# The small embedding of a graph recommender is added to the rows of x by GpSimd, in 26 pieces between steps of the sort

## The reference

```python
def _propagate(all_emb, rows, cols, vals):
    acc = all_emb
    x = all_emb
    for _ in range(N_LAYERS):
        x = jax.ops.segment_sum(vals[:, None] * x[cols], rows, num_segments=N_NODES)
        acc = acc + x
    return acc / (N_LAYERS + 1)
...
light_out = _propagate(all_emb, graph_rows, graph_cols, graph_vals)
mm_out = _propagate(mm_all, graph_rows, graph_cols, graph_vals)
users_emb = all_users[users] + _upsample_nearest(mm_users[users])
items_emb = all_items + _upsample_nearest(mm_items)
rating = users_emb @ items_emb.T + bias_user[users] + bias_item.T
return sigmoid(rating)
```

## Time and profile before

| | us |
|---|---|
| median of 3 runs | 5368.86 |
| lowest, highest | 5368.59, 5371.43 |
| profiled execution, its own time | 5364.2 |
| its span in the trace | 5362.3 |

### The profile page before, as it was taken

How to read it: one execution, slowest core, us unless ns; L and a number is a source line. 1 busy time by engine, 2 the same in 40 slices (tenths; PEclk the granted TensorE clock), 3 DMA queues, 4 the chain that set the end, 5 groups by cost and what they waited for, 6 DMA issues and landing times.

```text
span 5362.3 us, 195922 instructions
## 1 busy us (share of the span) xinstructions
PE 3360.9 (63%) x71235; PEld 2862.9 (53%) x71473; DVE 4779.3 (89%) x7551; ACT 2466.3 (46%) x4385; POOL 2473.0 (46%) x2179
## 2 busy tenths in 40 slices
PE   5600021111388888777688888867768888867767
PEld 4500011110377777666577777756657777766652
DVE  9989999999999999877899999967799999977778
ACT  0025555554466666500166666620046666640027
POOL 0038764433277777700067777720037777760000
PEclk9955555555699999999989999989989999989999
DMA  9960000300288877799978788889968877879999
GB/s 328 415 264 0 0 0 3 5 0 0 84 249 250 248 245 247 228 328 328 278 218 251 247 251 251 246 277 328 328 196 255 251 247 246 252 244 328 328 282 357
DMA packets 840271, 1191.20 MB, mean 222 GB/s; under 512 B 150791, under 2 KB 667582, under 8 KB 839824
## 3 DMA queue, kind: packets, MB, share of 16 engines
q1 hardware_dynamic: 716032, 816.66, 53.6%
q0 software_dynamic: 123872, 372.78, 18.2%
q10 hardware_dynamic: 304, 1.00, 0.1%
HBM read 638.35 MB, written 551.90 MB: 222 GB/s over the span
## 4 chain that ended last, share of the span: by engine, by line
DVE 27%; DMA 27%; issue 21%; POOL 10%; PE 7%; ACT 5%; SPq 1%; DVEq 1%; POOLq 0%; another core or an unknown queue 0%; ACTq 0%
DMA ring<-posts 15%; POOL posts L803 9%; DMA posts<-ring 8%; DVE store L1092 6%; PE psum L1543 4%; DVE total L889 3%; DVE ring L1313 3%; DVE store L1070 3%; ACT new L711 3%; DVE store L1071 2%; DMA out<-new 2%; DVE new L1285 2%; DVE ring L1337 2%; PE psum L1519 2%; DVE ring L1298 1%
## 5 line engine op out<-in xcount | busy, mean ns | idle before, releaser
L803 POOL DMA_INDIRECT posts<-ring x1884 | 1851.0, 982 | 1554.2 <-DVE ring L1298 962.3
L1519 PE MATMUL psum<-store,ring 128*128 x45216 | 2088.8, 197 | 485.0 <-DVE ring L1313 450.5
L1519 PEld LDWEIGHTS psum<-store,ring 128*128 128x128 bf16 x45216 | 1818.2, 100 | 755.7 <-issue 576.7
L711 ACT ACTIVATE new<-new 128x512 bf16<-128x512 uint8 x1884 | 1067.8, 614 | 0.0
L1313 DVE TENSOR_SCALAR ring<-ring,lane_f 128x1024 bf16<-128x1024 bf16 x1884 | 963.1, 553 | 10.7 <-DMA ring<-lanes_d 9.5
L1337 DVE TENSOR_TENSOR ring<-ring,wide_lane 128x1024 bf16<-128x1024 bf16 x948 | 613.3, 689 | 299.7 <-ACT ring L722 299.7
L1298 DVE TENSOR_TENSOR ring<-new 128x1024 bf16<-128x1024 bf16 x942 | 652.5, 693 | 92.4 <-ACT new L711 63.3
L709 ACT ACTIVATE ring<-new 128x512 bf16<-128x512 bf16 x942 | 585.8, 622 | 297.2 <-DVE new L1285 292.3
L767 POOL TENSOR_TENSOR ring<-store 128x1024 f32<-128x1024 f32 x157 | 369.6, 2354 | 662.7 <-DVE store L1010 306.4
L1285 DVE TENSOR_TENSOR new<-psum,vals_m 128x512 f32<-128x512 f32 x942 | 644.5, 684 | 6.9 <-PE psum L1519 4.9
L1429 PE MATMUL psum<-ident,store 128*128 128x128 f32 x224 | 51.6, 424 | 725.9 <-DVE store L1071 725.9
(11 more groups left out here) (232 smaller groups left out, 2728.0 us busy)
## 6 DMA issues: line engine op xcount, KB each, us to landing
ring<-lanes_d SPq DMA_DIRECT2D x471, 512.0 KB
ring<-posts SPq DMA_DIRECT2D x240, 772.0 KB, 6.7
store<-posts SPq DMA_DIRECT2D x234, 772.0 KB, 6.7
posts<-store SPq DMA_DIRECT2D x2, 30880.0 KB, 166.7
posts<-store SPq DMA_DIRECT2D x2, 30108.0 KB, 128.5
out<-new SPq DMA_DIRECT2D x96, 500.0 KB, 8.5
posts<-ring POOLq DMA_INDIRECT x1884
store<-L_rec_bias_item SPq DMA_DIRECT2D x1, 3125.0 KB, 14.6
```

Of the source, the lines that this page charges most:

```text
L711: last = nc.scalar.activation(digits[s][:, k, :], scaled_byte[s][k], ACT.Copy, scale=scale)
L803: pool.indirect_dma_start(out=posts[:, :], out_offset=bass.IndirectOffsetOnAxis(ap=dring[:, h, c:c + 1], axis=0), in_=msg[:, n, :], in_off ...
L1519: last = pe.matmul(psum[:, d % 4, (n % 2 * BLOCK + b) * F:(n % 2 * BLOCK + b + 1) * F], of, xflat[:, bass.ds(at_d[c] * F + (k * XT + x * F ...
```

## The change

The five transfers of `mini` are issued by SyncE behind the dummy keys' reads instead of behind the large embedding, and `mini` lies at another place of the ring, over tables that have been read by then. VectorE no longer adds, nor zeroes mini's last tile. In steps 128 to 153 GpSimd adds 6 tiles a step behind its subtraction: 24 pieces of 6 tiles, one of 2 tiles (SMALLS is 25), and one with the 62 rows of the last tile. ScalarE waits for all 26 instead of one.

```diff
--- before.py
+++ after.py
@@ -64,6 +64,8 @@
 SPARE = CHUNKS * P + 1
 MARKS = SUPERS * (RUNS + 1)
 MARK_COLS = -(-MARKS // P)
+SMALL, SMALL_FIRST = 6, 128
+SMALLS = -(-(TILES - 1) // SMALL)
 MARK_FIRST, ROW_FIRST, ROW_NEXT, DEST_AT = 10, 114, 119, 124
 PIECE_P = [(P0, HALF, HALF + P0), (HALF, 2 * HALF, 0), (2 * HALF, ROWS_M, 2 * HALF)]
 
@@ -173,7 +175,7 @@
         hots = [total[:, 2 * T + s * hot_words:2 * T + (s + 1) * hot_words].bitcast(BF16) for s in range(2)]
         col_b = total[:, 7028:7028 + T // 2].bitcast(BF16)
         row_b = total[:, 8008:8008 + T // 2].bitcast(BF16)
-        mini = ring[:, 0:TILES * MINI].rearrange("p (t m) -> p t m", m=MINI)
+        mini = ring[:, 7048:7048 + TILES * MINI].rearrange("p (t m) -> p t m", m=MINI)
         bits_a = ring[:, 2400:2400 + T].bitcast(I32)
         bits_b = ring[:, 4400:4400 + T].bitcast(I32)
         value_no = ring[:, 6400:6400 + VALUES].bitcast(BF16).rearrange("p (v c) -> p v c", c=2)
@@ -480,12 +482,14 @@
             sp.dma_start(cols_i[P - 1:P, 0:LAST_E], cols[(P - 1) * T:NNZ].rearrange("(p t) -> p t", p=1)).then_inc(s_cols, 16)
 
             sp.wait_ge(s_blank, 4)
-            for dst, ue, ie, s in ((new3, emb_u, emb_i, s_emb), (mini, mm_u, mm_i, s_mini)):
+            def rows_of(dst, ue, ie, s):
                 sp.dma_start(dst[:, 0:UTILES - 1, :], ue[0:(UTILES - 1) * P, :].rearrange("(t p) f -> p t f", p=P)).then_inc(s, 16)
                 sp.dma_start(dst[0:U_LANES, UTILES - 1, :], ue[(UTILES - 1) * P:USERS, :]).then_inc(s, 16)
                 sp.dma_start(dst[U_LANES:P, UTILES - 1, :], ie[0:I_FIRST, :]).then_inc(s, 16)
                 sp.dma_start(dst[:, UTILES:UTILES + I_TILES, :], ie[I_FIRST:I_FIRST + I_TILES * P, :].rearrange("(t p) f -> p t f", p=P)).then_inc(s, 16)
                 sp.dma_start(dst[0:I_LAST, TILES - 1, :], ie[I_FIRST + I_TILES * P:ITEMS, :]).then_inc(s, 16)
+
+            rows_of(new3, emb_u, emb_i, s_emb)
 
             sp.wait_ge(s_blank, 5)
             sp.dma_start(places[0:CHUNKS * P, :].rearrange("(p c) o -> p (c o)", p=P), blank[:, 0:CHUNKS]).then_inc(s_noplaces, 16)
@@ -506,6 +510,7 @@
             halves = dummies_d.rearrange("o (p h e) -> (o p) h e", h=2, e=1024)
             for h in range(2):
                 sp.dma_start(b_raw.bitcast(I32)[h * HALF + B_FIRST:(h + 1) * HALF, :], halves[:, h, :]).then_inc(s_bload, 16)
+            rows_of(mini, mm_u, mm_i, s_mini)
 
             sp.wait_ge(s_tabled, 1)
             sp.dma_start(marks_at[0:1, 0:MARKS].rearrange("o (s w) -> (o s) w", w=W), mark_at_i[:, :]).then_inc(s_tabout, 16)
@@ -671,7 +676,7 @@
 
 
             act.wait_ge(s_decoded, 1)
-            act.wait_ge(s_x0, 1)
+            act.wait_ge(s_x0, SMALLS + 1)
             act.wait_ge(s_zeroed, 64)
 
             def cast_one(layer, q):
@@ -767,9 +772,23 @@
                 nc.gpsimd.tensor_tensor(greater[SUBS[n] % 2].rearrange("p (a c) -> p a c", c=low[0].shape[2]), low[0], high[0],
                                         ALU.subtract).then_inc(s_greater, 1)
 
+            def small_added(p):
+                rows_p = P
+                tiles = slice(p * SMALL, min((p + 1) * SMALL, TILES - 1))
+                if p == 0:
+                    pool.wait_ge(s_emb, 16 * 5)
+                    pool.wait_ge(s_mini, 16 * 5)
+                if p == SMALLS:
+                    rows_p, tiles = I_LAST, slice(TILES - 1, TILES)
+                to = new3[0:rows_p, tiles, :].rearrange("p t (m r) -> p (t m) r", r=F // MINI)
+                of = mini[0:rows_p, tiles, :].rearrange("p t (m o) -> p (t m) o", o=1)
+                nc.gpsimd.tensor_tensor(to, to, of.broadcast_to(list(to.shape)), ALU.add).then_inc(s_x0, 1)
+
             for n in range(SORT_STEPS):
                 if n not in OWN_MASK:
                     greater_of(n)
+                if 0 <= n - SMALL_FIRST <= SMALLS:
+                    small_added(n - SMALL_FIRST)
                 if n == MARK_FIRST - 1:
                     pool.iota(order_i, pattern=[[1, CHUNKS]], base=-OFFSET - RAISE, channel_multiplier=CHUNKS).then_inc(s_orders, 1)
                     pool.wait_ge(s_noplaces, 16)
@@ -836,8 +855,7 @@
             nc.vector.memset(cols_i[96:P, LAST_E:T], 0).then_inc(s_blank, 1)
             nc.vector.memset(loads[0][:, T:WIDE], 0.0)
             nc.vector.memset(loads[0][96:P, LAST_E:T], 0.0).then_inc(s_blank, 1)
-            nc.vector.memset(new3[:, TILES - 1, :], 0.0)
-            nc.vector.memset(mini[:, TILES - 1, :], 0.0).then_inc(s_blank, 1)
+            nc.vector.memset(new3[:, TILES - 1, :], 0.0).then_inc(s_blank, 1)
             nc.vector.memset(zeros[:, :], 0.0)
             nc.vector.memset(nothing[:, :], 0.0)
             nc.vector.memset(xparts[:, TILES, :, :], 0.0)
@@ -912,11 +930,6 @@
             link(nc.vector.tensor_tensor(bits_a, bits_a, bits_b, ALU.bitwise_or))
             link(nc.vector.tensor_tensor(real, real, bits_a, ALU.bitwise_or))
             nc.vector.memset(keys[0][:, T:WIDE], SENTINEL)
-            dve.wait_ge(s_emb, 16 * 5)
-            dve.wait_ge(s_mini, 16 * 5)
-            new4 = new[:, 0:TILES * F].rearrange("p (t r) -> p t r", r=F // MINI)
-            small = mini.rearrange("p t (f o) -> p (t f) o", o=1)
-            nc.vector.tensor_tensor(new4, new4, small.broadcast_to([P, TILES * MINI, F // MINI]), ALU.add).then_inc(s_x0, 1)
 
 
             dve.wait_ge(s_hotused, HIST)
@@ -950,7 +963,6 @@
             link(nc.vector.tensor_scalar(key_f[:, body:], key_f[:, body:], edges[0:SUPERS, 0:1], None, ALU.add))
             link(nc.vector.tensor_copy(key_n, key_f))
             nc.vector.tensor_scalar(key_n, key_n, 15, None, ALU.logical_shift_left).then_inc(s_dkeys, 1)
-            dve.wait_ge(s_x0, 1)
             nc.vector.memset(b_raw, SENTINEL).then_inc(s_dkeys, 1)
```

## The result

Seven runs of each kernel on one chip: 5388.39 us (5380.26 to 5391.28) with the change, 5372.22 (5368.59 to 5374.56) before; the ratio is 1.003, its interval 1.002 to 1.0039. The change makes the kernel about 16 us slower. The prediction had 17.8 us and 5386.7.

A forecast was written before the change was run, and what follows sets the result against it. DMA was taken to bound the kernel up to the wait ahead of step 11, VectorE the sort from there. Removal 0, move 0 and pieces +17.8 on the median 5368.86 gave 5386.7 us, range 5368 to 5400.

The forecast's parts named there:

- Removed, 9.94 us, worth 0: VectorE's addition before the sort: its 9.94 us only lengthen the wait ahead of step 11, from 15.21 to 25.15.
- Moved, net 0 between -9.3 and +2.8: SyncE's queue: zeroing starts about 12.2 us earlier, but the five transfers cost 12.2 ahead of the table writes; net 0.
- the price they had: Small embedding's five transfers in SyncE's queue: assumed to cost 12.2 us at the new place too, between 2.9 and 15.0.
- Pieces, 17.8 us: Steps 128 to 153: GpSimd's additions hold up VectorE's minimum or maximum, 19.8 us less 2.0 of idle time.
- 2.0 was to be the sign: Steps 128 to 153: minimum or maximum would show a median of 2.0 us instead of 1.2.
- I take 2.1 ns: Pieces: VectorE pays 2.1 ns an element, the rate at which GpSimd's subtractions held it in two rows.
- the lower bound of 1.63: Pieces: 1.63 ns an element from the fastest 1024-element subtraction, giving 13.4 us after the deduction.
- as deducted: After own-mask steps 130, 137, 147: VectorE's idle waits for ScalarE's copy absorb 2.0 us of the pieces' price.
- the upper bound, the whole duration: Pieces: VectorE pays GpSimd's full time, fixed part included, 23.3 us after the deduction.
- hidden pieces: Rival: pieces fit in GpSimd's 2.30 us idle time, chain unchanged, time as before, 5368.9 us; chance 0.09.
- the early table: Rival: mark table comes 9.3 us earlier; 5377.4 with pieces as priced, chance 0.06; faster with cheap pieces, chance 0.05.
- A time per element of twice the subtraction's for the repeated operand: Rival: GpSimd reads the pieces' repeated operand at twice the time per element, 39.5 - 2.0, total 5406 us; chance 0.08.

The follow-up runs named there:

- e1: Kernel before without VectorE's addition, small embedding loaded but never added: 5337.14 us against 5339.10 before, ratio 1.0.
- e3: Changed kernel with the addition in 7 pieces of up to 21 tiles plus the last tile, ahead of layout-turning steps' subtractions: 5341.98 us, ratio 1.001 to before.
- e6: Changed kernel with each piece ahead of its step's subtraction instead of behind; one profiled run, steps 128 to 153 take 150.39 us (133.93 before).
- e7: Changed kernel with each piece a GpSimd memset, writing only; one profiled run, steps 128 to 153 take 133.66 us (133.93 before).
- e8: Changed kernel with each piece a GpSimd copy reading one operand; one profiled run, steps 128 to 153 take 139.20 us (133.93 before).
- e2: Changed kernel without the 26 additions, leaving the late transfers and the missing VectorE operation: 5339.78 us against 5339.10 before, ratio 1.0003.
- e4: Changed kernel with the small embedding's five transfers issued behind the mark tables' reads: 5340.22 us against 5339.10 before, ratio 1.0004.
- e10: Kernel before, addition still on VectorE, with only the zeroing of posts issued behind the mark tables' reads: 5319.94 us against 5337.39 before, ratio 0.9969.
- e5: Changed kernel with pieces at the layout-turning steps and the small embedding loaded behind the mark tables' reads: 5342.95 us against 5350.16 before, ratio 0.9979.
- the eight kernels of that prefix: The changed kernel and the variants identical to it up to the start of step 11, which lies at 385.25 to 387.59 us (383.94 before).
- e9: Changed kernel with pieces at the layout-turning steps, small embedding behind the mark tables, zeroing of posts behind both: 5313.81 us against 5337.39 before, ratio 0.9957.

## Why the prediction was right

**Removed, 9.94 us, worth 0.** Right, and shown by e1: the wait took it all.

**Moved, net 0 between -9.3 and +2.8.** The direction of both halves was right, the sizes less so. The first transfer of the zeroing is issued 11.1 us earlier (37.81 against 48.91) and the queue is free of it 10.4 us earlier, not 12.2; the five transfers hold SyncE for 14.45 us, not 12.4. Step 11 is 1.3 to 3.7 us late, 2.8 in the first profile, which is the term's own upper bound. What was mis-sized is the price of the five transfers, taken as "the price they had" at another place in the queue. Why the place changes the price isn't shown.

**Pieces, 17.8 us.** The mechanism as said: each piece falls on the pair of minimum and maximum and shuts one of them out (e3, e6, e7, e8). The size was 13.95 us in the stretch. A maximum pays 0.67 (a median of 1.88 us, where 2.0 was to be the sign), where 0.81 was taken: the mis-sized term is "I take 2.1 ns", the rate of the subtractions. The pieces take 1.8 ns an element (from 0.87 us for 384 in e6 and 2.60 for 1344 in e3), between the lower bound of 1.63 and the value taken. In 21 steps the maximum pays. Ahead of the own masks two pieces run in a row, and the second falls on the maximum and the first on the minimum; in step 129:

```profile
992.33 2.69 POOL L785 TENSOR_TENSOR new<-new,ring 128x384 f32<-128x384 f32 x2
...
992.42 1.86 DVE L1082 TENSOR_TENSOR store<-store 128x1024 f32<-128x1024 f32 x1
...
994.21 1.88 DVE L1083 TENSOR_TENSOR store<-store 128x1024 f32<-128x1024 f32 x1
```

So three minima pay too: 0.66 in 129 and 146, and 0.36 in 136, where the piece begins 0.36 us ahead of the minimum, beside the end of a predicated copy. Together 21 x 0.67 + 2 x 0.66 + 0.36 + 0.22 (the piece of 2 tiles) = 16.0, and 2.0 of it came out of the idle time behind the own masks, as deducted: VectorE's waits for ScalarE's copy are gone, and between 982 and 1130 all that it waits for is TensorE, as before.

```profile
DVE store L1118 <- PE psum L1441: 1.2, 2, 0.6
```

A piece alone takes 0.87, so VectorE doesn't pay the whole of it either; the upper bound, the whole duration, was too high by that too.

**The sum.** 2.8 late at step 11 and 13.95 for the stretch are 16.8; the sort ends 15.5 later, because between steps 66 and 128 the changed kernel is 1.1 us quicker (325.1 against 326.2; e1 has 326.5 and e2 325.4, so this wanders by itself). The forecast of 17.8 is 16.2 in the medians. Too much for the pieces (17.8 for 13.95) and too little for the table (0 for 2.8) partly cancelled: that the sum came within 2 us is luck in part, the mechanism isn't.

Of the rivals, hidden pieces and the early table would have needed what e3 and e4 did on purpose. A time per element of twice the subtraction's for the repeated operand is excluded by e6's 0.87 us.

## What to carry to other kernels

Before work is moved off a busy engine, look for the next thing that engine waits for: here a queue of zero writes that nothing needed for another 1000 us held the mark tables back, and 9.94 us taken from VectorE only made its wait longer; reordering the queue was worth 17 us by itself and made the removal worth its 9.9 us in the sort. GpSimd's idle time beside VectorE instructions with two SBUF operands isn't free time: an addition there costs VectorE 1.8 ns an element, 0.67 of the 0.87 us that GpSimd takes for it. The same addition beside a predicated copy with its mask in PSUM, or beside the turns, where nothing stands behind it, costs nothing, and a memset costs nothing even beside those instructions.

## What was not expected of the hardware

GpSimd's two-operand add over whole contiguous rows with a repeated second operand runs at 1.8 ns an element, its subtraction of strided halves mostly at 2.1. The subtraction's own price goes by how finely its halves interleave: in the kernel before all five with runs of 1 or 2 elements (steps 45, 55, 56, 136 and 153) take 1.88 to 1.89 us for 1024 elements, and all with runs of 4 to 1024 that met nothing take 2.33 to 2.38. What makes the addition cheaper, operation or pattern, was not tried. And the price of issuing the same 1.2 MB load in 64-byte rows goes by its place in the queue: 11.8 to 12.4 us behind the large embedding (before, e1, e10), 14.0 to 14.6 ahead of the table writes (the eight kernels of that prefix), 13.2 to 13.4 behind the table reads (e4, e5, e9). In e9 only the table reads stand ahead of it, ahead of the table writes only the reads of the dummy keys; the cause of the difference is open.
